# Two more blocks of the first expert moved into the last steps of the tile pipeline of an attention and expert kernel

## What is computed

```python
x = x + attention(layernorm(x), ctx, mask)          # 2 x 1024 tokens of 256, 77 keys, 16 heads
h = x_n + layer_norm(x_n) @ attn_w.T                # x_n = layernorm(x)
t = layer_norm(h)
top_vals, top_idx = top_k(t @ gate_w.T, 2)          # 8 experts, two for each token
comb[token, expert] = softmax(top_vals)
for e in range(8):
    oe = (silu(t @ gate_proj[e].T) * (t @ up_proj[e].T)) @ down_proj[e].T    # inner width 1024
    out = out + comb[:, e:e+1] * oe
x = x + h + out
```

## Time and profile before

| | us |
|---|---|
| median of 3 runs | 586.43 (585.51 to 589.74) |
| the profiled execution | 586.9 |
| its span, first to last instruction | 585.3 |
| PE busy / DVE / ACT / POOL | 521.6 / 350.4 / 260.9 / 257.9 |
| mean granted clock of TensorE | 0.939 |
| last tile step to first block's product | about 198 to 219 |
| first block's product to the last | about 219 to 574 |

### The profile page before, as it was taken

One profiled execution on the slowest core, in us unless ns is written; L12 is line 12 of the kernel. 1 busy time (PEld: TensorE's weight loads), 2 busy tenths in 40 slices (PEclk: granted clock), 3 DMA queues, 4 the chain that ended last, 5 costly groups with the idle time before them and its releaser, 6 DMA issues.

```text
span 585.3 us, 14031 instructions
## 1 busy us (share of the span) xinstructions
PE 521.6 (89%) x3389; PEld 448.9 (77%) x3390; DVE 350.4 (60%) x805; ACT 260.9 (45%) x523; POOL 257.9 (44%) x429
## 2 busy tenths in 40 slices
PE   2579999999998639999998999999999999999992
PEld 1367888888887428888887888887888888978882
DVE  2877889888786447543468456438433465385630
ACT  0445757675654223232375254336232363466420
POOL 5251445555455574564433525443543434432222
PEclk9858979999898658999999999999999999999997
DMA  7730010101010146621101455360162101530000
GB/s 219 205 141 2 18 37 20 36 20 36 18 36 20 37 153 132 227 81 45 46 27 36 150 190 201 101 202 27 44 212 77 45 27 45 169 112 29 20 17 27
DMA packets 25607, 48.10 MB, mean 82 GB/s; under 512 B 10560, under 2 KB 18652, under 8 KB 25440
## 3 DMA queue, kind: packets, MB, share of 16 engines
q1 hardware_dynamic: 15552, 33.55, 18.0%
q0 software_dynamic: 7360, 13.19, 7.4%
q10 hardware_dynamic: 2656, 0.91, 0.7%
HBM read 39.30 MB, written 9.39 MB: 83 GB/s over the span
## 4 chain that ended last, share of the span: by engine, by line
PE 73%; DVE 10%; issue 6%; POOL 3%; ACT 3%; DMA 2%; SPq 0%; POOLq 0%; DVEq 0%; ACTq 0%
PE psum L1305 18%; PE psum L1306 17%; PE psum L1307 17%; PE psum L1354 5%; PE psum L1202 4%; PE psum L1186 4%; DVE s_max L867 2%; PE psum L1225 2%; PE psum L1181 2%; DMA wk<-in_wkT 2%; DVE s_sb L873 1%; PE psum L1260 1%; PE psum L1324 1%; PE psum L1219 1%; ACT tT L768 1%
## 5 line engine op out<-in xcount | busy, mean ns | idle before, releaser
L1305 PE MATMUL psum<-split_w,tb_hi 128*128 x288 | 117.6, 408 | 6.6 <-issue 5.9
L1306 PE MATMUL psum<-split_w,tb_hi 128*128 x288 | 113.3, 393 | 0.0
L1307 PE MATMUL psum<-split_w,tb_lo 128*128 x288 | 113.2, 393 | 0.0
L1305 PE MATMUL psum<-split_w,aT_hi 128*128 x288 | 84.3, 293 | 3.2 <-DVE aT_lo L1129 3.1
L687 POOL DMA_INDIRECT out_x<-o_sb,add_at x36 | 36.4, 1012 | 110.8 <-DVE o_sb L1121 107.7
L1306 PE MATMUL psum<-split_w,aT_hi 128*128 x288 | 81.3, 282 | 0.0
L1307 PE MATMUL psum<-split_w,aT_lo 128*128 x288 | 81.2, 282 | 0.0
L1129 DVE TENSOR_TENSOR aT_lo<-psum,aT_hi 128x512 fp32r<-128x512 f32 x72 | 46.3, 684 | 55.9 <-ACT aT_hi L813 55.9
L843 DVE TENSOR_TENSOR split_w<-split_w (+1 forms) x48 | 56.1, 1218 | 31.8 <-ACT split_w L792 31.8
L1305 PEld LDWEIGHTS psum<-split_w,tb_hi 128*128 128x128 f32 x288 | 54.8, 190 | 18.2 <-issue 8.5
L1307 PEld LDWEIGHTS psum<-split_w,tb_lo 128*128 128x128 f32 x288 | 54.5, 189 | 11.5
(11 more groups left out here) (175 smaller groups left out, 957.9 us busy)
## 6 DMA issues: line engine op xcount, KB each, us to landing
split_w<-in_experts SPq DMA_DIRECT2D x28, 768.0 KB
split_w<-in_experts SPq DMA_DIRECT2D x1, 3072.0 KB
x_sb<-in_x SPq DMA_DIRECT2D x8, 256.0 KB, 5.5
z_rows<-rows SPq DMA_DIRECT2D x16, 128.0 KB, 1.7
out_x<-x_sb SPq DMA_DIRECT2D x16, 128.0 KB, 1.8
mask_raw<-in_mask ACTq DMA_DIRECT2D x2, 308.0 KB, 12.1
blk<-lists POOLq DMA_DIRECT2D x36, 1.0 KB, 2.1
rows<-z_rows,gather_at POOLq DMA_INDIRECT x36, 3.1
```

The costliest lines, as they stand in the source:

```text
L1305: nc.tensor.matmul(dst, hi, w_hi, start=first, stop=False)
L1306: nc.tensor.matmul(dst, hi, w_lo, start=False, stop=False)
L1307: return nc.tensor.matmul(dst, lo, w_hi, start=False, stop=last)
```

## The change

SOON goes from 3 to 4 blocks and SOON_TILES from 13 to 9: the lists of the first four blocks of expert 0 are taken when nine tiles are scattered, by SP instead of POOL, and POOL waits for them in step 17 before it scatters tile 9. Rows 0 and 1 are gathered at the end of step 17, the sums of blocks 0 and 1 at the end of step 18, rows 2 and 3 in steps 20 and 21. Stores of zeros to the rows of the seven last tiles go out before the pipeline on SP, so that gathers of unused list entries read defined rows.

Blocks 0 and 1 are worked inside steps 18 to 21: rows_T of both in step 18, both halves of block 0's gate and up in 19, block 1's first half, block 0's transposes and block 1's second half in 20, block 0's down product and rows_T of block 2 in 21, each behind the tile work of that step on PE, with ACT's and DVE's parts to match. For the banks of PSUM that they take, the logits and ranks of tiles 13 to 15 move to others. The weights (softmax) of tile 13 are computed a step earlier on ACT, those of tile 14 together with tile 15's in step 22, so tile 14's scatter comes with them. The blocks' pipeline then begins at its step 3, and row_table and block_tables stand in step 3, due_tables in 4. An expert 0 has at least FIRST_BLOCKS = 6 blocks, and BLOCKS grows from 42 to 45.

The diff, cut to its core (the rest renames, makes functions of the blocks' parts, and moves declarations):

```diff
-SOON, SOON_TILES = 3, 13
-BLOCKS = FULL_BLOCKS + EXPERTS - 1 + SOON
+SOON, SOON_TILES, FIRST_BLOCKS = 4, 9, 6
+BLOCKS = FULL_BLOCKS + EXPERTS - 1 + FIRST_BLOCKS
 USUAL_BLOCKS = FULL_BLOCKS + EXPERTS // 2
...
+LAST = TILES - 1
+DRAIN = LAST + PROJ - MIX
...
         mix_bank, o_bank, h_bank, qx_bank, proj_bank = bank[3], bank[4], bank[5][:, 0:D], bank[6], bank[7][:, 0:D]
...
-                if isinstance(n, int) and not 1 <= n - back_ < BLOCKS:
+                if isinstance(n, int) and not FIRST_BLOCKS - 1 <= n - back_ < BLOCKS:
...
+                if number_is(t, SOON_TILES):
+                    sp.wait_ge(pad_out, 16 * (1 + TILES - SOON_TILES))
+                    sp.wait_ge(blank_out, 16 * (TILES - SOON_TILES))
...
+                if number_is(t, SOON_TILES + SCATTER - LN2 - 1):
+                    soon_lists()
...
+            def soon_lists():
+
+                for par in range(2):
+                    sp.wait_ge(listed[par], 16 * TOPK * ((SOON_TILES + 1 - par) // 2))
+                for n in range(SOON):
+                    sp.dma_start(blk[:, n], lists[n * P:(n + 1) * P, :]).then_inc(soon_in, 16)
+
+            for t in range(SOON_TILES, TILES):
+                sp.dma_start(z2_tiles[t // 2, t % 2], zeros[:, :]).then_inc(pad_out, 16)
+                sp.dma_start(out_tiles[t // 2, t % 2], zeros[:, :]).then_inc(blank_out, 16)
 
             pipeline(sp, store, SOON_TILES, TILES - SOON_TILES, 0)
...
                 if number_is(t8, SOON_TILES):
-                    soon_rows()
+                    pool.wait_ge(soon_in, 16 * SOON)
                 if within(t8, TILES):
...
-                if number_is(t8, SOON_TILES - 1):
-                    soon_lists()
+                if number_is(t8, SOON_TILES):
+                    soon_rows()
+                if number_is(t8, SOON_TILES + 1):
+                    soon_sums()
+                if number_is(t5, LAST):
+                    pool.wait_ge(z2_out[0], 16 * TILES // 2)
+                    pool.wait_ge(tT_ps, TILES - 1)
+                    gather_rows(2, 2)
+                if number_is(t6, LAST):
+                    pool.wait_ge(z2_out[1], 16 * TILES // 2)
+                    pool.wait_ge(tT_ps, TILES)
+                    gather_rows(3, 3)
...
-            def soon_lists():
-
-                for par in range(2):
-                    pool.wait_ge(listed[par], 16 * TOPK * ((SOON_TILES + 1 - par) // 2))
-                for n in range(SOON):
-                    load_list(n, n * P)
-
             def soon_rows():
 
-                pool.wait_ge(pad_out, 16)
+                pool.wait_ge(pad_out, 16 * (1 + TILES - SOON_TILES))
                 for par in range(2):
                     pool.wait_ge(z2_out[par], 16 * ((SOON_TILES + 1 - par) // 2))
+                pool.wait_ge(xnT_ps, TILES)
+                pool.sem_inc(pool_met, 1)
                 for n in range(SOON):
-                    pool.wait_ge(blk_in[n], 16)
-                    pool.sem_inc(pool_met, 1)
                     nc.gpsimd.tensor_copy(gather_at[:, n, :], blk[:, n, 0:1]).then_inc(at_done, 1)
-                for n in range(SOON):
-                    if n == 2:
-                        pool.wait_ge(z2_out[0], 16 * TILES // 2)
-                        pool.wait_ge(tT_ps, TILES - 1)
+                for n in range(2):
                     gather_rows(n, n)
+
+            def soon_sums():
+
+                pool.wait_ge(so_far_zero, 1)
+                pool.wait_ge(acc_soon, 16 * SOON_TILES)
+                pool.wait_ge(blank_out, 16 * (TILES - SOON_TILES))
+                for n in range(2):
+                    nc.gpsimd.tensor_copy(add_at[:, n, :], blk[:, n, 0:1]).then_inc(add_at_done, 1)
+                for n in range(2):
+                    wait_apart(pool, add_at_done, n + 1, pool_met)
+                    gather_sums(n)
...
-
-            pool.wait_ge(so_far_zero, 1)
-            pool.wait_ge(acc_soon, 16 * SOON_TILES)
-            for n in range(2):
-                nc.gpsimd.tensor_copy(add_at[:, n, :], blk[:, n, 0:1]).then_inc(add_at_done, 1)
-            for n in range(2):
-                wait_apart(pool, add_at_done, n + 1, pool_met)
-                gather_sums(n)
...
+                if number_is(t3, LAST):
+                    rows_T(early[0])
+                    rows_T(early[1])
+                if number_is(t4, LAST):
+                    second_weight(back(it, MIX))
+                    gated(0, early[0])
+                    gated(1, early[0])
+                if number_is(t5, LAST):
+                    gated(0, early[1])
+                    acts_T(early[0])
+                    gated(1, early[1])
+                if number_is(t6, LAST):
+                    rows_T(early[2])
+                if number_is(t7, LAST):
+                    second_weight(back(it, LIST + 1))
+                    second_weight(t7)
...
+                if number_is(t5, LAST):
+                    gated(0, early[0])
+                    gated(1, early[0])
...
+                if number_is(t4, LAST):
+                    rows_T(early[0])
+                    rows_T(early[1])
...
+                if number_is(t7, LAST):
+                    first_weight(back(it, LIST + 1))
+                if within(t7, TILES) and not number_is(t7, LAST - 1):
...
+                if number_is(t7, LAST):
+                    other_weight(back(it, LIST + 1), TILES)
+                    other_weight(t7, TILES)
+                elif within(t7, TILES) and not number_is(t7, LAST - 1):
+                    other_weight(t7, n)
...
+                if number_is(t5, LAST):
+                    acts_T(early[0])
+                    gated(0, early[1])
+                    gated(1, early[1])
+                if number_is(t6, LAST):
+                    rows_T(early[2])
...
+                    acts_T(c)
+                if number_is(it, 3):
+                    row_table()
                 if has(b):
-                    for half in range(2):
...
-                if has(a) and not number_is(it, 1):
+                    gated(0, b)
+                    gated(1, b)
+                if has(a):
...
-                if number_is(it, 0):
-                    rows_T(back(it, -1))
-                    row_table()
-                if number_is(it, 1):
+                if number_is(it, 3):
                     block_tables()
-                if number_is(it, 2):
+                if number_is(it, 4):
                     due_tables()
...
-            pipeline(dve, experts_, USUAL_BLOCKS, 3, 4, GATHERS)
+            pipeline(dve, tiles, TILES, LIST, SCATTER + 2, begin=QK)
+            pipeline(dve, experts_, USUAL_BLOCKS, 3, 2 * GATHERS, GATHERS, 3)
...
+                    if number_is(t6, DRAIN):
+                        pe.wait_ge(tb_done, 2 * KD)
+                    transposed(rows_bank(t6), z2[:, t6[1], :]).then_inc(tT_ps, 1)
...
+                if number_is(t3, LAST):
+                    rows_T(early[0])
+                    rows_T(early[1])
...
-            pipeline(pe, tiles, TILES, LIST, SCATTER)
-
-            pe.wait_ge(s_done, 2 * TILES)
-            pe.wait_ge(place_done, TILES)
+                if number_is(t4, LAST):
+                    pe.wait_ge(s_done, 2 * TILES)
+                    pe.wait_ge(topi_done, DRAIN)
+                    pe.wait_ge(w_ready, PARTS)
+                    pe.wait_ge(tbl_done, 1)
+                    gate_up(0, early[0], first_weights())
+                    gate_up(1, early[0], first_weights())
+                if number_is(t5, LAST):
+                    pe.wait_ge(tbl_done, 2)
+                    gate_up(0, early[1], first_weights())
+                    pe.wait_ge(h_done, TILES)
+                    pe.wait_ge(place_done, DRAIN)
+                    acts_T(early[0])
+                    gate_up(1, early[1], first_weights())
+                if number_is(t6, LAST):
+                    pe.wait_ge(x1_done, TILES)
+                    pe.wait_ge(place_done, LAST)
+                    down(early[0], first_weights())
+                    pe.wait_ge(topi_done, TILES)
+                    rows_T(early[2])
...
+                    acts_T(c)
+                if number_is(it, 3):
+                    pe.wait_ge(before_done, TILES)
+                    pe.wait_ge(y_done, 1)
+                    nc.tensor.matmul(small[1], ones[:, :], before[:, 0, :], start=True, stop=True).then_inc(cnt_ps, 1)
...
+                if number_is(it, 3):
+                    pe.wait_ge(tab, 1)
                 if has(c):
...
+                    down(c, slot_at(c))
+
+            pipeline(pe, tiles, TILES, LIST, SCATTER)
+            pipeline(pe, experts_, USUAL_BLOCKS, 2, 2 * GATHERS, GATHERS, 3)
```

188 lines of the change are left out of this document (103 added, 85 removed).

## The result

The changed kernel takes 602.77 us (median of 4 runs, 601.41 to 603.92) beside 587.16 for the kernel before: a ratio of 1.0274, 95% interval 1.0236 to 1.0313. Forecast were 594.4, so the direction was right and the loss was 15.6 us instead of 8.0. The profiled execution took 602.71, with a span of 601.1 and a mean granted clock of 0.934.

The account below looks back on a forecast made before the run. POOL's chain of scatter, landing, list and gathers, not PE, was taken to end the change of phase. 586.9 + 0.4 (landing) + 1.8 (clock) + 5.8 (branches) = 594.9, less 0.5 to the median: 594.4 us; range 588 to 600.

Parts of the forecast that it names:

- Step 1: POOL's waits and added work in steps 17 to 19 delay the end of tile 13's logits from 198.16 to 200.6 us.
- Steps 2 to 4: Drain, steps 19 to 21, at full clock: block 2's gates start at 223.9 us instead of 236.09, 12.2 gained on PE.
- rival B: Drain runs at half clock: +8 us put straight on the last scatter, 602 us; chance 0.15.
- What is late instead: Last scatter at 230.0 us, table's first list 237.1, block 2's weighing 261.0, block 3's down product 262.4: +0.4 (−1.6 to +2.5).
- step 5: Table's DVE chain, ahead of block 2's products, through at 236.0 us; PE waits 2.4 before block 3; 9.8 gain left.
- Clock +1.8: Nine matmuls at half clock after PE's idle before block 3's down product: +1.8 us (0 to 2.9).
- The end +5.8: Three more absent blocks branched over at PE's end, 1.93 us each: +5.8 us (2.8 to 10).
- rival C: Kernel's end: branches are cheap, three cost 2.2 us, time 590.8, no change to be told; chance 0.12.
- The range: Whole kernel, from the bounds for landing, clock and branches: 588 to 600 us; for eight in ten 581 to 603.
- The rest of the blocks only moved: Behind block 3's down product POOL stays ahead of PE's 9.45 us a block, so later blocks are only moved.
- Rival A: Change of phase: POOL doesn't bind, PE's 9.8 us stay, 582.4 us (579.4 with cheap branches); chance 0.2.

Follow-up runs that it names:

- e1: Changed kernel with only 6 of the 9 absent blocks asked for at the end: 596.68 us, ratio 1.0171.
- e5: Changed kernel with block 2's gather of sums just behind the last scatters, without waiting for block 0's addition to land (four address columns, later landing waits): 596.91 us.
- e4: Changed kernel with short unused products of two constants in PE's waits of the last tile steps: 600.8 us, ratio 1.0244.
- e6: e5 with the constant products of e4 added: 589.04 us, ratio 1.0022.
- e8: e4 with one more wait on SP, so the weight loads of experts 1 and 2 begin only when block 2's sums are gathered: 594.79 us, ratio 1.0133.
- e3: Changed kernel with ACT's second weights (tiles 14 and 15) put ahead of the copies of block 2's transposed rows: 603.18 us, ratio 1.0319.

## Why the prediction had the right direction and was 8 us short

- *Step 1 (POOL in steps 17 to 19)*: held. The logits of tile 13 ended at 199.55, forecast 200.6. Counted from SP's store ahead of it (171.42, before 172.74) they are 2.7 us later than before, forecast 2.4. That this execution's tile phase ran 1.3 ahead is not the change's doing: e1 and e5, with the same tile phase, have this store at 172.68 and 173.46.
- *Steps 2 to 4, the failed step.* They were worked out "at the full clock". Block 0's gates took 7.2 us instead of 5.5, block 1's gates with block 0's transposes 9.2 instead of 6.4 (211.82 to 221.04), block 0's down product 4.2 instead of 2.95 (223.29 to 227.53), the logits 0.4 more. Together 6.2, and block 2's gates came at 229.99, not 223.9. From block 0's first gate product to block 2's the forecast had 23.3 us, the changed kernel took 29.85, and e4, e6 and e8, at the full clock, 23.9 to 24.0: the instructions were counted nearly rightly and their rate was wrong. What was overlooked: the half-rate products at 219.81 in the earlier trace rows come behind a stretch in which PE mostly waited, and each of these three blocks also came behind such a stretch. They were used for the one idle before block 3's down product and not for the drain. The argument held against rival B, "from the gates on PE is busy", was true of block 0's gates and no help: the clock read 0.50 from 200.7 to 204.1 with PE busy throughout.
- *Rival B* had 0.15 and 602 us. Its cause is what came. That its time came too is in part luck: it put +8 on the last scatter, which was 6.5 behind the forecast; the rest of the 8.4 between forecast and median is 0.6 at the end, 1.2 in later blocks, and the base.
- *What is late instead.* The chain was named link by link and each link is in the trace, the idle of PE before block 3's down product among them. Its +0.4 was mis-sized; it measured +6.7: the last scatter came at 236.47, not 230.0 (+6.5), the list at 244.14, not 237.1 (+7.0), block 2's weighing at 267.39, not 261.0 (+6.4), the product at 268.73, not 262.4. The interval from list to weighing, forecast 23.9, was 23.25, the landing 5.9 for 5.4. The delay of the drain went through the chain undiminished in this execution, as rival B said ("put straight on the last scatter").
- *The table* (step 5) came at 241.7, not 236.0, and PE's wait for it was 2.69 us, forecast 2.4. As a second hold on the list it was not in the sum: 236.0 and the 1.75 seen in e1 and e3 are 237.8, against 237.1.
- *But the clock alone would not have made it right.* With it (e4) the time is 600.8. From the last scatter to the list were 8.4 us (landing 6.6), forecast 7.1, and list to product took 28.4 instead of 25.3. Only with the weight loads held back as well (e8) do list (236.17), idle (7.98), product (261.84) and time (594.79) stand where the forecast had them (237.1, some 8, 262.4, 594.4), and the forecast had these loads under way. So with a faster PE the landings took longer than the sum had them, which is a second miss; its cause is shown only in part.
- *Clock +1.8* behind the idle: block 3's down product began at the half rate, and from its start to the next gates it was 4.6 us (268.73 to 273.29) where 2.9 were usual (262.02 to 264.96): +1.6. Held.
- *The end +5.8*: 6.4 in the trace, 6.1 taken back by e1. Held; rival C (cheap branches) is out.
- *The range* of 588 to 600 was closed too early: the upper ends of its own terms add up to 601.8.
- *The rest of the blocks only moved*: nearly. 1.2 us were lost behind 273.29, most of them around 319 to 328, where PE's wait for a split of activations is 2.60 us and was 1.88; why was not tried.
- *Rival A*: POOL does bind, most of all where PE is fast: in e4 PE waits 9.88 us for it, about the 9.8 that the forecast expected to be thrown away. With that chain out of the way and the clock kept (e6), PE's first flag load comes at 572.3, 1.1 us ahead of the kernel before, and only the tests at the end keep the kernel from being faster.

So the 15.6 us are 6.4 of three more tests on PE's queue, 8.3 of the late chain with the half-rate products behind it, and 1 of small shifts. The two extra blocks in the drain gained nothing, because what they freed on PE was waited away, and what they put in the way of the last tiles' ranks and weights delayed the scatters on which POOL's chain hangs. Of the 14.6 us of that delay (221.91 to 236.47) 5.2 went with the clock (e4) and 3.6 with the place of ACT's second weights (e3), each edit by itself; the rest is the blocks' own work.

## What to carry to other kernels

Before moving work of a busy engine into a hole, follow what else leaves the hole: here the last tiles' lists passed through it, and the serial chain of another engine's queue (scatter, landing, list, gather, add, gather of sums) started from them. Work put into a hole is to be priced at the rate that the hole's own rows show, not at the steady state's, and a gain on one engine (5 us at the last scatter in e4) can be worth 2 until the queue that ends the stage is shortened too, and then 8. One wait of such a chain was 2.71 us in one execution and 5.45 in another of the same code, so one trace of each kernel doesn't tell what an edit did to it; the medians do. A test for an optional block isn't free at the end of a program: nested tests cost one jump, and the second engine in line says how much of it can be had.

## What was not expected of the hardware

- A taken branch on PE's queue over code that isn't run took 0.21 to 2.85 us, and one jump over six or nine bodies 3.72 and 3.75 us; the same branches took 0.045 on ACT and 0.056 on DVE in the same kernels. From six to nine bodies the price didn't grow.
- The granted clock was 1.00 from 206 to 234 us with 8 to 24 products of two constants in PE's waits (e4), and block 2's gates started at 224.82 instead of 229.99; without them all of block 1's first half ran at 0.50, and the clock fell to 0.50 within block 0's gates while PE was busy.
- A scatter of 128 rows to DRAM held the queue that waited for its landing 2.71 us in the changed kernel's trace and 5.45 in e1's, whose program is the same up to that place.
